# Low parts of the gates' weight quarters moved to a turn's last step and the next turn's first five, the weights' loads behind them

## The reference

```python
x = x + layernorm(S4(layernorm(x)))
x = x + layernorm(FFN(layernorm(x)))
# S4: a causal convolution per channel, as product of spectra, then an exact gelu
K  = dplr_kernel(B, C, P, Q, Lam, step)          # 512 channels, 64 states
h1 = irfft(rfft(r, 4096) * rfft(K, 4096))[:2048]
y  = gelu(h1 + D * r)
# FFN: a gated recurrence without output gate over the 8 sequences (the scan), then a head
f, i = sigmoid(x @ wf.T + c @ uf.T + bf), sigmoid(x @ wi.T + c @ ui.T + bi)
g = tanh(x @ wc.T + c @ uc.T + bc)
c = f * c + i * g
h = tanh(x @ wo.T + c_final @ uo.T + bo)
```

## Time and profile before

| | us |
|---|---|
| median of 3 runs (lowest, highest) | 2779.64 (2774.74, 2779.66) |
| profiled execution, its own time | 2779.75 |
| its span, first to last instruction | 2777.9 |
| of it before the convolution, convolution, after | 137, 482, 2159 |
| PE busy, share of the span | 2591.0, 93% |
| DVE, ACT, POOL busy | 1941.2, 1511.5, 959.8 |
| mean granted clock of PE | 0.972 of full speed |

### The profile page before, as it was taken

One profiled execution on the slowest core, in us unless ns is written; L12 is line 12 of the kernel. 1 busy time (PEld: TensorE's weight loads), 2 busy tenths in 40 slices (PEclk: granted clock), 3 DMA queues, 4 the chain that ended last, 5 costly groups with the idle time before them and its releaser, 6 DMA issues.

```text
span 2777.9 us, 54870 instructions
## 1 busy us (share of the span) xinstructions
PE 2591.0 (93%) x21507; PEld 2101.9 (76%) x21507; DVE 1941.2 (70%) x3404; ACT 1511.5 (54%) x2802; POOL 959.8 (35%) x1449
## 2 busy tenths in 40 slices
PE   4499999996799999999998989999999999999998
PEld 4277877884588888888886878888888888644443
DVE  7865666546776767776777777777677765478778
ACT  6655556564555555555555555555555554345444
POOL 7777676622221222121222222212221210144445
PEclk9799999997899999999999999999999999999999
DMA  9878787788445534543554564455355434288777
GB/s 329 290 222 292 261 287 243 259 308 273 121 107 131 124 100 109 133 121 96 118 139 124 113 169 100 106 130 127 96 109 138 116 96 111 95 295 282 263 255 265
DMA packets 524548, 489.94 MB, mean 176 GB/s; under 512 B 275584, under 2 KB 406912, under 8 KB 519040
## 3 DMA queue, kind: packets, MB, share of 16 engines
q1 hardware_dynamic: 524288, 486.43, 59.5%
HBM read 270.60 MB, written 150.73 MB: 152 GB/s over the span
## 4 chain that ended last, share of the span: by engine, by line
PE 80%; DVE 8%; DMA 4%; ACT 3%; issue 2%; POOL 1%; SPq 1%; DVEq 0%; POOLq 0%; ACTq 0%
PE bank L1909 28%; PE bank L1919 27%; PE bank L1977 12%; PE bank L1749 3%; PE bank L1799 3%; PE bank L1785 2%; PE bank L1807 2%; DVE big L1432 2%; PE bank L1961 1%; DMA big<-yd 1%; PE bank L1761 1%; DMA big<-big 1%; DMA big<-xr 1%; DVE big L1344 1%; PE bank L1769 1%
## 5 line engine op out<-in xcount | busy, mean ns | idle before, releaser
L1909 PE MATMUL bank<-big 128*128 128x256 f16 x8064 | 1098.5, 276 | 73.0 <-ACT big L1156 29.2
L1919 PE MATMUL bank<-big 128*128 128x256 f16 x7056 | 965.3, 273 | 0.0
L1909 PEld LDWEIGHTS bank<-big 128*128 128x128 f16 x8064 | 796.3, 99 | 184.4 <-ACT big L1156 32.4
L1919 PEld LDWEIGHTS bank<-big 128*128 128x128 f16 x7056 | 691.7, 98 | 81.1
L883 POOL TENSOR_SCALAR big<-big 128x1 f32<-128x1 f32 x256 | 55.7, 217 | 1308.5 <-DVE big L1456 785.4
L1977 PE MATMUL bank<-big 128*128 128x512 f16 x1536 | 332.2, 379 | 0.0
L1137 ACT ACTIVATE big<-big 128x512 f32<-128x512 f32 x384 | 290.9, 805 | 62.4 <-DVE big L1626 61.9
L1626 DVE TENSOR_TENSOR big<-bank,big 128x512 f32<-128x512 f32 x192 | 131.4, 684 | 228.4 <-PE bank L1919 218.2
L1977 PEld LDWEIGHTS bank<-big 128*128 128x128 f16 x1536 | 150.3, 98 | 181.2
L1050 ACT ACTIVATE big<-big 128x512 f32<-128x512 f32 x256 | 206.6, 807 | 116.3 <-POOL big L885 115.5
L1172 ACT ACTIVATE big<-bank 128x512 f32<-128x512 f32 x192 | 113.9, 593 | 260.8 <-PE bank L1919 251.8
(11 more groups left out here) (209 smaller groups left out, 3594.2 us busy)
## 6 DMA issues: line engine op xcount, KB each, us to landing
big<-xr SPq DMA_DIRECT2D x16, 2048.0 KB, 11.1
big<-xg SPq DMA_DIRECT2D x64, 512.0 KB, 6.7
big<-kpad SPq DMA_DIRECT2D x32, 1024.0 KB, 12.4
yd<-big SPq DMA_DIRECT2D x16, 2048.0 KB, 17.3
big<-x SPq DMA_DIRECT2D x128, 256.0 KB, 3.2
x1d<-big SPq DMA_DIRECT2D x128, 256.0 KB, 2.0
xtd<-big SPq DMA_DIRECT2D x64, 512.0 KB, 4.9
big<-xtd SPq DMA_DIRECT2D x64, 512.0 KB, 4.5
```

Of the source, the lines that this page charges most:

```text
L1909: ins = e.matmul(o, WX[2 * g + lw][:, q, kt, 128 * a:128 * a + 128], slot[u % 2][:, part, lx, k0 + kt, :], start=(first and kt == 0 and (l ...
L1919: ins = e.matmul(o, WC[2 * g + lw][:, q, kt, 128 * a:128 * a + 128], cc[unit(u)[1] % 2][:, qc, lx, kt, :], start=False, stop=end, skip_gro ...
```

## The change

In turns 2, 3, 6, 7, 10 and 11 the high parts keep their steps. The low parts, which stood in steps 9 to 15, one step or none behind their high parts (in turn 2 from step 10 on, with the last in the next turn's step 0), go to new places: parts 0 and 1 to step 15 of the turn, parts 2 to 6 to steps 0 to 4 of the next turn. The two stores go with parts 3 and 6, to steps 1 and 4 of the next turn. The loads of the matrices 3, 4, 7, 8, 11, 12 and 15 move from the start of their turn (step -1, for 3 step 0) to step 5. The four `most` of the matrices 4, 8 and 12 move from steps 7 to 10 to steps 9 to 12. PE's, ACT's and POOL's queues keep their order.

```diff
-            at[n, {2: 3, 3: 0}.get(n, -1)].append(("load", n, 0))
+            at[n, 3 if n == 2 else 5 if n % 4 in (0, 3) else -1].append(("load", n, 0))
             if n % 4 < 2:
-                places = [("most", f, n, 7 + f) for f in range(4)]
+                places = [("most", f, n, (7 if n % 4 else 9) + f) for f in range(4)]
...
                 places = [("hi", q, n, min(first + q + (q > 2 and n > 2), 15)) for q in range(7)]
-                places += [("lo", q, n + (first + 1 + q) // 16, (first + 1 + q) % 16) for q in range(7)]
+                places += [("lo", q, n, 15) for q in range(2)] + [("lo", q, n + 1, q - 2) for q in range(2, 7)]
```

## The result

The changed kernel takes 2832.21 us (median of 4 runs, 2826.7 to 2837.83), the kernel before beside it 2779.65 (4 runs, 2774.74 to 2779.93): a ratio of 1.0197, 95% interval 1.0179 to 1.0215. It is slower by 52.6 us; forecast were 2835 and a range of 2803 to 2860. The profiled execution of the changed kernel took 2833.94 us, its span 2832.1, at a mean granted clock of 0.965.

What follows compares the result with a forecast made beforehand. PE bounds the convolution, with 24.0 us of waiting to be won in the touched turns, about 2 more in turn 2. Pairs +54.1, turns 2, 6, 10 -7.7, turn 15 +9.0: +55.4, so 2835 us, range 2803 to 2860.

Steps and rivals of the forecast that it cites:

- Low parts held by POOL: Steps 0 to 4: parts 3 to 6 each meet a POOL instruction; 4.8 us lost in turns 3, 4, 7, 8, 11, 12.
- The upper bound of 7.6: Early loss in turns 4, 8 and 12 with one more POOL period, if POOL still has last turn's work: 7.6 us.
- The landing: The weights' load, behind part 6, its store and `yd`, lands 13.5 us after part 6, 28.9 us into the turn.
- The load in time: Rival, 4%: the load overtakes `yd` and the stores, landing before step 8; only POOL's 4.8 us remain; 2783 us.
- The waits: PE delayed by the late load: 6.8 us in turns 3, 7, 11; 4.2 in 4, 8, 12; 7.0 in 15.
- The clock: PE's clock falls behind each wait: 2.0 us in turns 3, 7, 11, 15 and 1.5 in 4, 8, 12.
- The sum: Three pairs 245.7 us (+54.1), turns 2, 6, 10 -7.7, turn 15 +9.0; total +55.4 us.
- POOL is missed: Rival, 10%: POOL starts later than the low parts, which cost nothing, but the load lands near 24; 2806 us.
- Both: Rival, 3%: low parts free and the load in time, so all waits go, -26.0 us; 2754 us.
- POOL's leftovers: Bound only: POOL's work left from the last turn costs 2.8 us more in each of three turns, +8.4 us.

Runs made afterwards that it cites:

- load_ahead_of_yd: The changed kernel with the load of the weights issued in step 5 ahead of the `yd` store on SP's queue; 2795.81 us.
- pe_kept_busy: The changed kernel with 50 or 40 unread products on PE ahead of the states it waits for, in the seven waits for the load; 2830.1 us.
- pool_sliver: The changed kernel with POOL's normalising instructions cut to 16 numbers of a partition in place of 1024 from turn 3's `xg` loads on; 2810.73 us.
- load_ahead_of_store: The changed kernel with the loads ahead of part 6's store and `yd`, and matrix 15's load back at its turn's start; 2786.43 us.
- second_of_pair: The kernel before with low parts of turns 3, 7, 11 moved, and in turns 4, 8, 12 `xg`, loads and `most` moved too; 2774.37 us.
- idle_pool_earlier_rows: The changed kernel with turns 4, 8, 12's low parts in steps 2 to 8, `xg` there behind part 2, loads and `most` moved too; 2771.03 us.

## Why the prediction was right

The time came out 2.8 us under the forecast, and each of the three mechanisms showed in the trace at its place. By its steps:

- **Low parts held by POOL, 4.8 us a turn.** Turn 7: part 6 ends 15.5 us in (15.4 said), and PE takes up the state behind it at 358.88, 15.9 in (15.9 said). Taking from each turn's length 28.87 and what its late steps lost, the early loss was 3.0, 4.8, 4.8, 5.0, 5.1 and 4.6 us in turns 3, 4, 7, 8, 11 and 12. Turn 3 is the exception: POOL came 4.6 us into the turn there, part 3 began 0.04 us ahead of it and took 0.74, and it was POOL's instruction that took longer (2.97 for 2.38). The upper bound of 7.6 did not come here, but it did in load_ahead_of_yd.
- **The landing, 28.9 us into the turn.** 29.2 in turn 7. The order of issue held, as the earlier trace rows had it. The rival in which the load overtakes `yd` fell with load_ahead_of_yd too: it is the place in the queue that decides. The Trainium skill (DMA: Bandwidth & Descriptors, "Queues, rings and completion order") says that completion is not first in, first out; in the traces of the twelve kernels here no load or store landed ahead of one that was issued before it.
- **The waits.** Idle time of PE in turns 3, 7 and 11: 7.1, 7.0 and 5.7 us (6.8 said); in 4, 8 and 12: 4.1, 4.3 and 4.5 (4.2 said); in 15: 6.3 (7.0 said, as the load landed 28.1 and not 28.6 in).
- **The clock.** What the late steps lost beyond the idle time: 2.2, 2.8 and 2.5 us in turns 3, 7 and 11 and 1.7 in turn 15 (2.0 said), and 3.1, 1.5 and 3.1 in turns 4, 8 and 12 (1.5 said). This agrees with half the busy time at the lower clock: 2.7, 1.35 and 3.0 in turns 7, 8 and 12. It is the term that was mis-sized, in two turns by half: I took a shorter wait to cost a shorter time at the lower clock, but in turn 12 PE worked 6.0 us at 0.50, longer than behind the longest wait (4.2 us behind the 7.1 of turn 3); turn 8 with 2.7 is the exception. All seven sum to 16.7 us against 12.5 said. pe_kept_busy shows that these steps are the clock's, and also that the term can't simply be taken off the sum.
- **The sum.** The pairs 248.2 (245.7 said), turns 2, 6 and 10 together -7.7 (-7.7 said), turn 15 +8.0 (+9.0 said). At the start of turn 16 +56.6, in the profiled executions +54.2 (55.4 said). The sum came closer than its terms, and that is in part luck: the clock's 4.2 us too few stand against 1.5 too many in the early loss, 1.0 in the waits, and the 2.4 us after the convolution, which no term had.
- **The rivals.** "POOL is missed" was priced at 2806 and pool_sliver, which makes it so, took 2810.7. "The load in time" was priced at 2783 and load_ahead_of_store, which nearly makes it so, took 2786.4. "Both" at 2754 was not reached by any kernel: the best took 2771.0.

One coupling the prediction had only as a bound ("POOL's leftovers", 8.4 us). Its sum took turns as if each stood alone; but POOL's work per turn is fixed, so whatever shortens the first turn of a pair lets POOL's leftovers reach the low parts of the second. The changed kernel's long turns mostly hid that, and three of the experiments paid for it. In load_ahead_of_yd and second_of_pair it is why the time was 10 and 8 us above the expected; in pe_kept_busy, also 10 above, it is a part of the gap, and the rest is open.

## What to carry to other kernels

When a load is moved in a hand-written order, count what is ahead of it on its queue, and look at what its issuing engine must wait for there: here one part that was held on DVE kept the DMA engines empty for 2 us, and then 2.75 MB went ahead of the weights. A short instruction that shares time with another engine's long ones belongs where that engine is idle, and that place moves when a turn gets shorter, so look at the turn behind before adding gains up.

## What the runs showed of the hardware

- A low part that takes 0.74 us alone took 2.0 to 2.8 (parts 3 to 6 of the changed kernel) when it began during one of POOL's instructions of 2.4 us, and ended some 0.55 us after that instruction. POOL's next instruction, which had begun by then, took 2.71 to 2.83 in place of 2.4. In turn 3, where the low part began first, it was free and POOL's instruction took 2.97. With POOL's instructions cut to a sliver the low parts took 0.75.
- Behind an idle time of 4.1 to 7.1 us PE worked at 1.2 GHz for another 2.7 to 6.0 us, and four products of L1798 took 1.06 us in place of 0.61. With PE kept at work during the wait the clock stayed at 2.4 GHz. In turn 8 it was 2.7 us behind an idle time of 4.3, in turn 12 6.0 behind 4.5; the runs don't show what sets the difference. Shorter idle times, of 2.0 to 2.6 us, let the clock fall in some turns and not in others: 2.03 in turn 8 of pe_kept_busy did, 2.04 in its turn 4 did not.
- The low parts read two operands from SBUF, the `most` one, and a `most` ran in 0.68 us while POOL's instruction ran from 385.03 to 387.42. But one input is no safeguard: the TENSOR_SCALAR of L1425 took 1.95 us beside POOL, and 0.48 without it in idle_pool_earlier_rows.
